# Query, key and value biases leave TensorE, and the row sums leave ScalarE, in a one-core transformer layer

## The reference

```
q = split_heads(x @ Wq + bq); k = split_heads(x @ Wk + bk); v = split_heads(x @ Wv + bv)
q = p / (sum(p) + EPS)  with  p = exp(q - max(q))          # per head of 16 features; k likewise
context = ((q @ k.T) / (sum(q) + EPS)) @ v                 # no softmax over tokens: linear attention
x = layernorm(x + context @ Wo + bo)
gate, up = fp4(x) @ fp4(w_gate).T, fp4(x) @ fp4(w_up).T    # blocks of 16 rounded to a 4-bit grid
x = layernorm(x + fp4(silu(gate) * up) @ fp4(w_down).T)
```

## Time and profile before

| | |
|---|---|
| median of 3 executions | 774.97 us (774.73 to 778.72) |
| profiled execution, its own time | 774.18 us |
| its span in the trace | 772.2 us |
| PE busy | 720.7 us (93%) |
| PEld busy | 684.2 us (89%) |
| DVE busy | 662.2 us (86%) |
| ACT busy | 573.8 us (74%) |
| POOL busy | 575.9 us (75%) |
| granted TensorE clock, mean | 0.987 of full speed |

### The profile page before, as it was taken

The page is one execution under the profiler, slowest core; times in us unless marked ns, Lnnn a source line. Parts: engine busy times, 40 slices in busy tenths (PEclk is TensorE's granted clock), DMA queues, the critical chain, the costliest instruction groups (busy, mean ns, idle before and its releaser), DMA issues.

```text
span 772.2 us, 17178 instructions
## 1 busy us (share of the span) xinstructions
PE 720.7 (93%) x4964; PEld 684.2 (89%) x4964; DVE 662.2 (86%) x1492; ACT 573.8 (74%) x1547; POOL 575.9 (75%) x617
## 2 busy tenths in 40 slices
PE   4999999999999978699999989999989999989984
PEld 3899998998999867599999989999989999989984
DVE  5988899889889985899899899899899898997784
ACT  3577777887887787467777767777767778778877
POOL 4677667676676675678878878888878888888861
PEclk9999999999999989899999999999999999999998
DMA  4222222222222100000000000000000000001112
GB/s 129 69 74 75 72 77 75 64 72 68 83 76 63 50 26 2 1 2 1 1 1 1 2 1 22 18 20 21 22 14 22 21 15 22 22 14 42 42 42 95
DMA packets 39768, 29.81 MB, mean 39 GB/s; under 512 B 3446, under 2 KB 39676, under 8 KB 39676
## 3 DMA queue, kind: packets, MB, share of 16 engines
q1 hardware_dynamic: 37228, 26.50, 11.4%
q10 hardware_dynamic: 2448, 2.23, 1.0%
HBM read 20.32 MB, written 8.39 MB: 37 GB/s over the span
## 4 chain that ended last, share of the span: by engine, by line
PE 47%; DVE 26%; issue 15%; POOL 5%; ACT 4%; DVEq 1%; DMA 1%; POOLq 0%; ACTq 0%; SPq 0%
PE bank L854 30%; PE wide L854 5%; POOL scratch L418 4%; DVE scratch L842 4%; PE bank L916 3%; DVE scratch L778 3%; PE bank L862 3%; DVE scratch L784 3%; DVE scratch L829 2%; PE wide L903 2%; PE bank L914 2%; PE wide L957 1%; DVE scratch L763 1%; DVE scratch L795 1%; DVE scratch L813 1%
## 5 line engine op out<-in xcount | busy, mean ns | idle before, releaser
L854 PE MATMUL bank<-wf_hi,rounded 128*128 128x352 f32 (+1 forms) x1792 | 408.6, 311 | 21.8 <-DVE rounded L835 8.3
L854 PEld LDWEIGHTS bank<-wf_hi,rounded 128*128 128x128 f32 x1792 | 301.4, 190 | 30.9 <-DVE rounded L835 14.0
L854 PE MATMUL bank<-wf_lo,rounded 128*128 128x352 f32 (+1 forms) x896 | 274.0, 306 | 0.0
L854 PEld LDWEIGHTS bank<-wf_lo,rounded 128*128 128x128 f32 x896 | 170.7, 190 | 0.0
L418 POOL TENSOR_TENSOR scratch<-scratch 128x704 f32<-128x704 f32 x64 | 93.0, 1452 | 76.6 <-DVE scratch L809 76.5
L854 PE MATMUL bank<-qkv_hi,rounded 128*128 128x512 f32 (+1 forms) x512 | 146.1, 340 | 0.0
L854 PEld LDWEIGHTS bank<-qkv_hi,rounded 128*128 128x128 f32 x512 | 93.5, 192 | 10.0
L402 POOL TENSOR_TENSOR scratch<-scratch 128x704 bf16<-128x704 f32 x64 | 98.9, 1545 | 2.2 <-ACT scratch L591 2.2
L584 ACT ACTIVATE scratch<-scratch 128x704 uint8<-128x704 f32 x64 | 50.6, 791 | 63.6 <-POOL scratch L418 63.4
L360 POOL TENSOR_TENSOR scratch<-scratch 128x512 f32<-128x512 f32 x64 | 68.1, 1064 | 36.9 <-DVE scratch L710 36.8
L425 POOL TENSOR_TENSOR scratch<-scratch 128x704 f32<-128x704 bf16 x64 | 89.1, 1392 | 5.8 <-DVE scratch L813 0.7
(11 more groups left out here) (102 smaller groups left out, 1657.7 us busy)
## 6 DMA issues: line engine op xcount, KB each, us to landing
scratch<-x_feat SPq DMA_DIRECT2D x64, 128.0 KB, 2.3
scratch<-x_tok SPq DMA_DIRECT2D x64, 128.0 KB, 2.1
out<-scratch SPq DMA_DIRECT2D x64, 128.0 KB, 1.7
scratch<-w_ffn ACTq DMA_DIRECT2D x17, 128.0 KB, 2.2
scratch<-L_attn_Wq SPq DMA_DIRECT2D x1, 256.0 KB, 3.0
scratch<-L_attn_Wk SPq DMA_DIRECT2D x1, 256.0 KB, 3.2
scratch<-L_attn_Wv SPq DMA_DIRECT2D x1, 256.0 KB, 3.9
wo<-L_attn_Wo SPq DMA_DIRECT2D x1, 256.0 KB, 3.1
```

The costliest lines, as they stand in the source:

```text
L854: last = pe.matmul(dst, x(c), w(c), start=first and n == 0, stop=n == len(terms) - 1)
```

## The change

Four things are done.

1. The bias matmuls of q, k and v go. `bias_b` holds the three biases broadcast over the 128 partitions, loaded by DMA. For q and k ACT writes the bias of a tile into its PSUM bank (`seed`) and the six matmuls add onto it, none of them starting a new group. Four matmuls ahead of the loop (`opened`) write both banks once, so that later matmuls accumulate. For v POOL adds the bias to `v_sb` in SBUF after ACT has copied it (`a_vb`), and PE's key-value product waits for that.
2. The row sums of both layer norms come from the accumulator output of DVE's residual additions, which become `scalar_tensor_tensor`. ACT's row-sum and minus-mean instructions go, the squares read the sum itself (scale -256), and the variance is divided by 256 cubed instead of 256.
3. The start is reordered: the first tile of x is loaded and split before the weights, DVE no longer waits for POOL's constants or makes `bias_r`, POOL sets only the identity and the mask before the rest.
4. `seed(m+1)` stands on ACT behind the exponential of tile m-1.

```diff
@@ loads (SyncE)
             loads(0, [0])
-            for k, b in enumerate((bq, bk, bv)):
-                sp.dma_start(bias_f[0:33:32, k * D:(k + 1) * D],
-                             b.rearrange("(a n) -> a n", a=1).broadcast_to((2, D))).then_inc(ld_bias, 16)
-            loads(0, [1, 2])
+            weights(0, Wq)
+            weights(1, Wk)
+            bias(0, bq)
+            bias(1, bk)
+            weights(2, Wv)
+            loads(0, [1])
+            bias(2, bv)
+            loads(0, [2])
...
@@ attention (GpSimd)
+                    if live(i, t, -1):
+                        b1 = (t - 1) % 2
+                        if (i, t) == (0, 1):
+                            pool.wait_ge(ld_bias[1], 16)
+                        need(pool, a_v, m)
+                        pool.tensor_tensor(v_sb[b1], v_sb[b1], bias_b[:, 2 * D:3 * D], ALU.add).then_inc(a_vb, 1)
...
@@ (ScalarE)
+            def seed(n):
+                act.activation(pqk[n % 2][:, :], bias_b[:, 0:2 * D], ACT.Copy).then_inc(a_seed, 1)
+            x_hi_step(0)
+            weights_hi(0)
+            weights_hi(1)
+            act.wait_ge(ld_bias[0], 32)
+            act.wait_ge(opened, 1)
+            seed(0)
+            weights_hi(2)
+            act.wait_ge(opened, 2)
+            seed(1)
+            x_hi_step(1)
-            def row_sums(n, norm, ready, sm):
...
-                act.activation(dump[:, 0, :], res[:, rows(n)], ACT.Copy, accum_out=row_sum[:, at]).then_inc(sm, 1)
-            def minus_mean(n, norm, sm, nm):
...
-                act.activation(row_nm[:, at], row_sum[:, at], ACT.Copy, scale=-1.0 / D).then_inc(nm, 1)
-                act.activation(dump[:, 1, :], res[:, rows(n)], ACT.Square, bias=row_nm[:, at],
+                act.activation(dump[:, :], res[:, rows(n)], ACT.Square, bias=row_sum[:, at], scale=-1.0 * D,
                                accum_out=row_sq[:, at]).then_inc(sq, 1)
...
                         act.activation(prob[b1][:, :, 0:HD], prob[b1][:, :, 0:HD], ACT.Exp).then_inc(a_exp, 1)
+                    if m >= 1 and live(i, t, 1):
+                        need(act, a_sub, m)
+                        seed(m + 1)
...
@@ (VectorE)
-            dve.wait_ge(consts, 5)
...
-            dve.wait_ge(ld_bias, 48)
-            dve.tensor_copy(bias_r[0:1, :], bias_f[0:1, :]).then_inc(bias_s, 1)
-            dve.tensor_copy(bias_r[32:33, :], bias_f[32:33, :]).then_inc(bias_s, 1)
...
-                        dve.tensor_tensor(res[:, rows(m - 7)], po[:, 0:D], x_bo[(t - 7) % T],
-                                          ALU.add).then_inc(a_res, 1)
+                        dve.scalar_tensor_tensor(res[:, rows(m - 7)], po[:, 0:D], 1.0, x_bo[(t - 7) % T], ALU.mult, ALU.add,
+                                                 accum_out=row_sum[:, m - 7:m - 6]).then_inc(a_res, 1)
...
-                        dve.tensor_tensor(res[:, rows(m - 5)], pd[:, 0:D], res[:, rows(m - 5)],
-                                          ALU.add).then_inc(y_s, 1)
+                        dve.scalar_tensor_tensor(res[:, rows(m - 5)], pd[:, 0:D], 1.0, res[:, rows(m - 5)], ALU.mult, ALU.add,
+                                                 accum_out=row_sum[:, NT + m - 5:NT + m - 4]).then_inc(y_s, 1)
...
@@ (TensorE)
+            pe.wait_ge(consts, 5)
+            for b in range(2):
+                for c in range(2):
+                    last = pe.matmul(pqk[b][:, c * D:(c + 1) * D], ident[:, :], mask[:, :, :],
+                                     start=c == 0, stop=True, skip_group_check=True)
+                last.then_inc(opened, 1)
             pe.wait_ge(wq_lo_s, 2)
-            pe.wait_ge(bias_s, 3)
-            def qkv(dst, t, lo, hi):
-                pe.matmul(dst, ones_r[:, :], bias_r[:, lo:hi], start=True, stop=False)
+            def qkv(dst, t, lo, hi, first):
...
-                        need(pe, a_sub, m - 1)
-                        qkv(pqk[b][:, :], t, 0, 2 * D).then_inc(a_qk, 1)
+                        need(pe, a_seed, m + 1)
+                        qkv(pqk[b][:, :], t, 0, 2 * D, first=False).then_inc(a_qk, 1)
...
+                        need(pe, a_vb, m - 1)
                         need(pe, a_feat, m - 1)
```

101 lines of the change are left out of this document (42 added, 59 removed).

## The result

| | before | after |
|---|---|---|
| time, us (median, 6 runs each) | 775.4 (774.29 to 778.72) | 769.34 (768.84 to 770.27) |
| span of the profiled execution, us | 772.2 | 767.4 |

The ratio is 0.9918, with a 95% interval of 0.9898 to 0.9938. The change makes the kernel faster by 0.8%, 6 us; forecast were 755 us and a range of 747 to 765. The sign was right, the size was not.

The account below looks back on a forecast made before the run. PE was taken to bound attention, busy 188.8 of 190 us. Terms -22.4 + 4.5 + 2.5 - 3.7 - 0.7 = -19.8 us took 774.18 to 754.4, given as a 755 us median; range 747 to 765.

Parts of the forecast that it names:

- Bias matmuls, -22.4 us: Attention on PE: removing 0.35 us of bias matmuls from each of 64 tiles saves 22.4 us.
- What is lost of the 22.4 us: Attention: 4.5 us lost in layer-norm groups and 2.5 us in small waits elsewhere; bounds 0 and 16 us.
- POOL, +0.74: Attention: the value-bias addition adds 0.74 us per tile to POOL, 3.58 us of a 3.71 us period.
- DVE, +0.09: Residual addition: the accumulating form adds 0.09 us per tile to DVE in attention, 3.61 us of 3.71.
- the third rival: Attention: DVE and POOL limit the period to 3.96 us through blocked two-input DVE instructions; 764 us, chance 0.20.
- ACT, +0.03: Attention: a 0.63 us seed replaces 0.60 us of row-sum work per tile; ACT needs 3.22 us of 3.71.
- The start, -3.7 us: Kernel start: PE's first matmul begins at 7.0 us instead of 10.71, gaining 3.7 us.
- FFN 0 and end -0.7: FFN stage unchanged, the longer residual being hidden; at the end, removed ACT steps before the layer norm gain 0.7 us.
- The change of stage, 0,: Between attention and FFN: left as it is, since ACT's saving may be taken by the added wait on POOL.
- DVE and POOL set the pace: Rival: in attention, locked small two-input DVE instructions hold the period at 3.96 us, not 3.71; 764 us, chance 0.20.
- It doesn't do what it says: Rival: seeds come late, so the bias matmuls' time returns as PE waiting; only start and end gain; 771 us, chance 0.05.
- the third case: Rival with DVE and POOL limiting attention; its sign was a period near 4.0 with POOL over 95% busy; chance 0.20.

Follow-up runs that it names:

- v_pe_dve: Changed kernel with value bias as PE matmul again; in each sequence's last tile DVE's residual addition precedes the head sums and `w_g` follows them; 762.15 us.
- no_vb: Changed kernel without POOL's value-bias addition and its waits, so the value bias is missing from the result; 764.02 us.
- seed_late: Changed kernel with ACT's seed for the next tile moved behind the rounding of the features of the tile after next; 768.65 us.
- vb_twice: Changed kernel with a second POOL addition of the same shape per tile, into a buffer that nothing reads; 794.74 us.
- rowsum_only: Kernel before with only the row sums taken from the accumulator of DVE's residual additions, biases still matmuls on PE; 773.07 us.
- bias_first: Changed kernel with the query and key bias loads ahead of the three weight loads; 770.17 us.

## Why the prediction was wrong, point by point

*Bias matmuls, -22.4 us.* The size was nearly right: 4 x 0.35 = 1.40 us per cycle were forecast, and 16.39 - 15.16 = 1.23 is what PE can give back when nothing else is in its way. v_pe_dve splits it: 16.39 - 15.48 = 0.91 for the 512 columns (0.92 forecast). For the 256 columns 0.32 are left of 0.48; either a little waiting is hidden in PE's rows or the matmul behind the transposes pays part of it, which I can't tell.

*"What is lost of the 22.4 us", +7.0 us: the step that failed.* It measured 21.9 (-0.5 in place of -22.4). I had put all four engines within 0.5 us of each other by their sums (3.71, 3.61, 3.58, 3.22) and allowed 4.5 us for the layer-norm tiles and 0.05 us a tile, 2.5 us, for all others. Against 1.40 us forecast for each cycle, the three layer-norm cycles lost 3.9 us, so that part was about right. The ten quiet ones lost 12.1 and the two at the start 4.4: the 2.5 us were the wrong term. For the sums weren't the limit. In the kernel after, POOL is busy 166.1 of 190 us and ACT 151.9, and still the cycle is 16.07: it is a circle over three engines, made of waits that each look small. Even the bound of 16 us was too low, since it took 0.25 us per tile from averages.

*POOL, +0.74.* The price was right (748 ns), the place was not. I noted that x_lo, `x_bo` and `feat` stand behind the addition and then let it fit since 3.58 is under 3.71. Removed, it gives 5.3 us, with DVE reordered 8.9. In the second cycle of the kernel it alone makes the growth from 15.05 to 15.98 us: without it (no_vb) that cycle lasts 15.00.

*DVE, +0.09.* Wrong, and harmless: the accumulator read takes 81 ns and the next instruction starts with it (152.45 and 152.45 above), the residual stays at 412 ns. What I left out on DVE was larger: 0.85 us for `w_g`, which had happened to miss `feat` before. I had seen the hold twice, in the layer-norm stretch and in the FFN, and booked it only there; the third rival priced it for the small instructions alone.

*ACT, +0.03.* Right in sum (592 ns in place of 630), and no wait for the seed shows from 60 to 250 us. seed_late shows that its place ahead of x_hi costs about 0.7 us, which is within the noise.

*The start, -3.7 us: 2.2.* The bias of k took 5.4 us to land, not 3.4: the price came from the load of `bo_b`, and here three 256 KB loads of weights ran beside it. That these are the reason is argued; no run tests it. Loading the biases ahead of the weights made PE start later still.

*FFN 0 and end -0.7* were right: from one L425 to the next but one are 14.03 us, as before, and at the end 1.23 us lie between the residual and the layer-norm step, for 2.06 before. *The change of stage, 0,* gave 1.2 us, which no run takes apart.

```profile
759.19 0.42 DVE L773 SCALAR_TENSOR_TENSOR res<-bank,res 128x256 f32<-128x256 f32 x1 [1.70 <-PE bank L855]
...
760.42 0.17 DVE L621 TENSOR_SCALAR ln_v<-row_sq 128x4 f32<-128x4 f32 x1 [0.80 <-ACT dump L480]
```

*The rivals.* "DVE and POOL set the pace" (764 us) was nearest in its mechanism: it named both engines, with the right reason, held two-input instructions. Its period of 3.96 was too short, because it too worked from averages per tile. "It doesn't do what it says" (771) was nearest in its total, by luck: PE's time did come back as waiting, but for the residual, not for seeds. The signal that I named for the third case, POOL over 95% busy, would have misled: POOL is at 87%, and at 95% only in vb_twice.

## What to carry to other kernels

When the bounding engine is about to lose several per cent, don't compare the others' sums with its new period; walk once round the cycle through every engine's list, from wait to wait, and add it up, for that circle is the next bound. Here it was within 2% of the old one (16.08 to 16.39 us) while no engine but PE was over 92% busy. Look at each wait in it for the branch that ends just ahead of it: what a cut can gain is the lead over that branch. An instruction added to an engine that waits a lot is free only while that circle has room: price it by putting a dummy into the kernel before, and look at every kind of cycle, not the common one. A VectorE instruction with two SBUF inputs that GpSimd's long ones now overlap, as `w_g` here, is part of the price.

## What the runs showed of the hardware

- The accumulating form of the residual addition (one PSUM and one SBUF input, 256 columns) costs nothing from start to start: 0.34 us to the accumulator read (152.11 to 152.45), the next instruction at the same time; quiet cycles of rowsum_only stay at 16.39 us.
- `w_g` with two bf16 SBUF inputs takes 0.28 us in the kernel before, where it starts as GpSimd's product `feat` ends, 1.13 us when it starts 0.09 us behind that product of 1.07 us, and 1.27 us in the other form. Its place in DVE's list was the same: a shift of about 1 us between the two engines made its row four times as long. A `tensor_scalar` with one SBUF input and 16 columns (L689) lasts 0.65 us too where it starts at 155.63, 0.11 us behind POOL's L373, and 0.16 us at its shortest.
- With two bias rows broadcast to 128 partitions ahead of it, a 256 KB weight took 5.9 us from issue to landing in place of 3.4 (bias_first against the kernel after).
